# A Gram matrix from high and low parts: one fp32 product replaced by three fp32r products, with the splits placed on ScalarE and VectorE ahead of the edge plan

## What is computed

```
xn = _layernorm(x, axis=-1)
x = x + _L0_gnn_ref(xn, edge_index, ...) + _L0_mix_ref(xn[None], w_qkv, w_out, b_out)[0]

def _L0_mix_ref(x, w_qkv, w_out, b_out):
    qkv = x @ w_qkv
    ...
    attn = jnp.einsum('bhnd,bhmd->bhnm', q, k) * (SCALE / n)
    out = jnp.einsum('bhnm,bhmd->bhnd', attn, v)
    ...
    return out @ w_out + b_out
```

## Time and profile before

| what | value |
|---|---|
| median of 3 runs | 908.46 us (906.35 to 911.83) |
| the profiled execution's own time | 909.68 us |
| its span, first to last instruction | 907.9 us |
| mean granted TensorE clock | 0.951 |
| PE busy | 803.0 us, 88% |
| VectorE busy | 630.3 us, 69% |
| ScalarE busy | 372.4 us, 41% |

### The profile page before, as it was taken

The page is one execution under the profiler, slowest core; times in us unless marked ns, Lnnn a source line. Parts: engine busy times, 40 slices in busy tenths (PEclk is TensorE's granted clock), DMA queues, the critical chain, the costliest instruction groups (busy, mean ns, idle before and its releaser), DMA issues. The chain is left out here.

```text
span 907.9 us, 11554 instructions
## 1 busy us (share of the span) xinstructions
PE 803.0 (88%) x4058; PEld 575.9 (63%) x4058; DVE 630.3 (69%) x1207; ACT 372.4 (41%) x557; POOL 102.4 (11%) x76
## 2 busy tenths in 40 slices
PE   5999999999999960895899998998797999999788
PEld 3777888888778840563587777555463445446564
DVE  7667776776749557598853232778867888884976
ACT  2342343332313240475112117756315887884150
POOL 3000000000000005012280004443100000000010
PEclk9989999999999995898599999999898999999999
DMA  5571312210302414996311102000001000000002
GB/s 173 150 250 49 107 56 71 71 36 8 117 1 92 147 65 138 286 373 233 97 66 47 47 22 72 1 1 1 2 2 48 1 1 1 1 0 1 6 1 93
DMA packets 48152, 66.63 MB, mean 73 GB/s; under 512 B 4268, under 2 KB 22460, under 8 KB 48095
## 3 DMA queue, kind: packets, MB, share of 16 engines
q1 hardware_dynamic: 43903, 56.22, 19.4%
q0 software_dynamic: 2384, 6.92, 2.3%
q10 hardware_dynamic: 1808, 2.75, 0.8%
HBM read 56.38 MB, written 9.50 MB: 73 GB/s over the span
## 5 line engine op out<-in xcount | busy, mean ns | idle before, releaser
L879 PE MATMUL bank<-xT,slot 128*128 128x512 f32 (+1 forms) x248 | 105.9, 427 | 5.7 <-DVE xT L1626 5.7
L880 PE MATMUL bank<-xT,slot 128*128 128x512 f32 (+1 forms) x248 | 98.5, 397 | 0.0
L881 PE MATMUL bank<-xT,slot 128*128 128x512 f32 (+1 forms) x248 | 98.2, 396 | 0.0
L1350 ACT ACTIVATE slot<-bank 128x512 fp32r<-128x512 f32 (+3 forms) x60 | 34.2, 586 | 144.3 <-PE bank L1129 56.3
L879 PE MATMUL bank<-slot 128*128 128x512 f32 (+1 forms) x212 | 85.2, 402 | 4.1 <-issue 1.8
L2131 DVE TENSOR_REDUCE key<-bank 128x2 f32<-128x1024 f32 x64 | 75.2, 1218 | 14.5 <-PE bank L1189 14.5
L879 PE MATMUL bank<-slot,xT 128*128 128x512 f32 (+1 forms) x192 | 79.2, 412 | 3.7 <-DVE arena L2194 2.8
L881 PE MATMUL bank<-slot 128*128 128x512 f32 (+1 forms) x212 | 81.9, 386 | 0.0
L880 PE MATMUL bank<-slot 128*128 128x512 f32 (+1 forms) x212 | 81.8, 386 | 0.0
L881 PE MATMUL bank<-slot,xT 128*128 128x512 f32 (+1 forms) x192 | 77.0, 401 | 0.0
L1563 ACT ACTIVATE arena<-bank 128x1024 f32<-128x1024 f32 x64 | 65.7, 1027 | 27.7 <-PE bank L1255 27.6
(11 more groups left out here) (323 smaller groups left out, 1647.5 us busy)
## 6 DMA issues: line engine op xcount, KB each, us to landing
arena<-in_ewT SPq DMA_DIRECT2D x16, 1024.0 KB, 11.5
arena<-in_edge_attr SPq DMA_DIRECT2D x16, 512.0 KB, 4.0
wraw<-in_qkvT SPq DMA_DIRECT2D x3, 1024.0 KB, 5.2
expert_rows<-rows SPq DMA_DIRECT2D x1, 2560.0 KB, 14.0
wraw<-in_L_ffn_expert_b POOLq DMA_DIRECT2D x16, 160.0 KB, 5.8
expert_results<-wraw ACTq DMA_DIRECT2D x16, 160.0 KB, 5.7
xn<-in_x SPq DMA_DIRECT2D x4, 512.0 KB, 6.3
wraw<-in_L_mix_w_qkv SPq DMA_DIRECT2D x2, 1024.0 KB, 7.8
```

Source lines behind the costliest of these rows:

```text
L879: pe.matmul(out, L[1], R[0], start=start, stop=False, **kw)
L880: pe.matmul(out, L[0], R[0], start=False, stop=False, **kw)
L881: return pe.matmul(out, L[0], R[1], start=False, stop=stop, **kw)
L1350: act.activation(h, src, kw.pop("func", ACT.Copy), **kw).then_inc(hi_done, 1)
```

## The change

A tile `xn_split` (high and low part of the normalised input, 128 x 2 x 8 x 512 fp32r) is laid over a part of the arena that is empty at that time. ACT copies each normalised tile into its high half, between and behind its square roots. DVE subtracts it for the low half: the pairs 0 and 1 inside the loop of moments, the pairs 2 and 3 after the last `normalise`, ahead of the edge plan. PE waits for a tile's low part before that tile's share of G, and makes the share in three fp32r passes with `mm3`. The transposes still read `xn`.

```
+        xn_hl = nc.alloc_sbuf_tensor_at("xn_split", [P, 2, T, D], F32R, offset=arena_at + 4 * AW)
...
             for t in range(T):
                 turn_rows(0, t)
+                pe.wait_ge(gram_lo, t + 1)
                 for m in range(C):
                     if t == 0:
                         open_bank("G", m)
-                    ins = pe.matmul(at("G", m)[:, m * P:D], xn[:, t, chunk(m)], xn[:, t, m * P:D], start=t == 0, stop=t == T - 1)
+                    ins = mm3(at("G", m)[:, m * P:D], [xn_hl[:, v, t, chunk(m)] for v in range(2)],
+                              [xn_hl[:, v, t, m * P:D] for v in range(2)], t == 0, t == T - 1)
...
-            for g in range(len(GROUPS[0])):
-                deviation(0, g)
+            for g in range(len(GROUPS[0]) + 1):
+                if g < len(GROUPS[0]):
+                    deviation(0, g)
+                for t in range(2 * g - 2, 2 * g) if g else ():
+                    act.wait_ge(xn_ready, t + 1)
+                    act.activation(xn_hl[:, 0, t, :], xn[:, t, :], ACT.Copy).then_inc(gram_hi, 1)
...
+            def gram_low(g):
+                for t in range(*GROUPS[0][g]):
+                    dve.wait_ge(gram_hi, t + 1)
+                    dve.tensor_tensor(xn_hl[:, 1, t, :], xn[:, t, :], f32(xn_hl)[:, 0, t, :], ALU.subtract).then_inc(gram_lo, 1)
+
             for t in range(T):
                 dve.wait_ge(x_in[t // 2], 16)
                 link(moments(t, xn[:, t, :]))
...
                     if t > 2:
                         normalise(0, t // 2 - 1, lambda t: xn[:, t, :])
+                    if t > 4:
+                        gram_low(t // 2 - 2)
             normalise(0, 3, lambda t: xn[:, t, :])
+            gram_low(2)
+            gram_low(3)
             dve.wait_ge(ids_in, 48)
```

More of the change, by code:

```diff
@@ L508, in build @@
         xn_ready = sem("xn_ready")
+        gram_hi = sem("gram_hi")
+        gram_lo = sem("gram_lo")
         masked = sem("masked")
```

## The result

| what | before | changed |
|---|---|---|
| first measurement: median of 10 executions each | 906.74 us | 910.20 us (908.34 to 912.44) |
| ratio, 95% interval | | 1.0031 [1.0017, 1.0045], +2.8 us |
| second measurement (12 of the changed kernel, 29 of before) | 907.25 us | 910.3 us, 1.0033 [1.0021, 1.0044] |
| span of the profiled execution | 907.9 us | 910.2 us |
| GT starts (profiled execution) | 35.27 us | 37.10 us |

A forecast was written before the change was run, and what follows sets the result against it. PE, busy 88% of the span, was taken to bound the kernel. Bank 0's wait of +3.0 us, less 0.87 and 0.19 from cheaper shares, gave +1.9 on the median of 908.46: 910.4 us, range 906.2 to 914.2.

The forecast's parts named there:

- DVE's queue: Eight low-part subtractions ahead of DVE's edge plan delay it and the emptying of bank 0 by 4.9 us, at most 5.5.
- The wait for bank 0: Tile 4's transposes wait for DVE's low part of xT 0, starting at about 27.25 us, 3.0 later than before.
- The share: A tile's share of G on PE in three passes costs 1.87 us, at most 2.03, instead of 2.16 in fp32.
- Hidden costs: Spans and DMA issues for mWv and mWo move 4.9 us later with DVE's queue, yet arrive before they are wanted.
- The sum: At GT's start: 3.0 - 0.87 - 0.19 = +1.9 us, so 37.2 instead of 35.27; up to +3.0 with dearer prices.
- The slow start: PE's first share starts at 15.05 instead of 11.79, at the lower clock until 21.0; bank 0's wait swallows both.
- B: Rival: PE alone, not bank 0, decides tile 4's start; -0.7 us at G's end, 907.8 us; chance 0.05.
- C: Rival: PE's 3 us gap behind the first transposes makes the clock rise much later; up to +15 us, 923; chance 0.04.
- E: Rival: a later wait for a DMA that does not move absorbs the delay; 908.5 us; chance 0.07.
- D: Rival: the 2 us shift removes or adds a low-clock stretch elsewhere; 907.5 or 913.3 us; chance 0.05 each way.

The follow-up runs named there:

- fp32 kept: Changed kernel with splits, waits and order kept, but PE multiplies plain fp32 xn instead of three passes; 1.0053 against before, +4.8 us.
- one pass: Changed kernel with only the high by high pass of the Gram matrix, splits and waits kept; one execution, 908.6 us.
- the queue alone: Kernel before plus eight unused 128x512 DVE subtractions between the last normalise and the edge plan, Gram matrix still fp32; 1.0086, +7.8 us.
- the version on POOL: Changed kernel with the eight low parts subtracted by POOL instead of DVE, ahead of its wait for the spans; 1.0026 against before, +2.4 us.

## Why the prediction was right, and the step that was too small

- **DVE's queue.** 4.9 us for eight subtractions; measured 4.82. The price per instruction that the prediction takes from the Trainium skill, "VectorE: DVE Perf Modes", section on the TRN2 errata, 5.5 us in all, was not the one.
- **The wait for bank 0.** Tile 4's transposes at 27.25; measured 27.20, in the changed kernel, with fp32 kept and with one pass. With the queue alone 27.65, in an execution that began 0.3 us late.
- **The share.** 1.87 us was worked out; measured 1.95, since the first 512-wide pass behind the transposes takes 0.31 us and not 0.23 and the 384-wide ones 0.18. The transposes became 0.05 us shorter, so that a tile is 2.33 us instead of 2.30. Three tiles gained 0.80 us where 0.87 was in the sum, and the last tile 0.30 where 0.19 was: two misses that cancel, by luck.
- **Hidden costs.** The spans and mWv moved by about 5 us, mWo's issue by 6.0 (25.39 to 31.43), and no row waits for them; ACT's copies lie in its idle time. These covers held.
- **The sum.** GT at 37.2; measured 37.10. +1.9 against that one profile; measured +1.83, that is 2.93 - 0.80 - 0.30.
- **The slow start was called hidden "whatever PE does until then".** True of the changed kernel. But the sum set it against one profile of before, in which the clock rose late (the first share took until 16.06, the second started at 16.91). In the others tile 2 started up to 1.3 us earlier. That step, the before side of the subtraction, was mis-sized: by the four profiles the sum should have said +1.8 to +3.2 at GT, centred on 2.5. The share of 4.3 us in the earlier trace rows, twice 2.16, showed that the clock rose only behind it there; what was missing was the thought that the change takes away PE's freedom to profit from an early rise.
- **Rivals.** B, C and E did not come about: PE did wait at tile 4, its clock was up by about 19.5, and the executions' times show the loss. D is real in both directions: both profiles of the changed kernel lack the low clock at 130 to 145 us, and the two have spans of 910.2 and 905.8 us with GT at the same time. L1976, at 340.99 in the first, starts at 338.69 in the second, whose window from 320 to 330 us has a clock of 1.00. The forecast held although D moved single executions by as much as the whole effect.
- **Not weighed for this wait.** The new wait before tile 4 could itself bring the clock down. The clock fell behind the waits of 4.07, 2.34 and 6.04 us, not behind those of 0.36, 1.04, 1.52 and also not behind 2.35 us (the version on POOL). The wait before M is 1.8 us in all fourteen profiles; the matmul behind it takes 0.76 or 0.77 us in seven and 0.47 in the other seven. So the length of the wait alone does not decide. Whether some executions of the changed kernel lose more that way, and so make up the rest between 2.5 and 2.8 to 3.0 us, is open; neither of its two profiles shows it, and the intervals hold 2.5.

## What to carry to other kernels

Before making an engine's work cheaper, find the next wait on its path and count what the helpers of the change add in front of that wait's releaser: here 1.1 us of cheaper matmuls behind the wait stood against 3 us of queue before it. If the helper work must be paid, put the releases that others wait for ahead of it, and leave the first tiles, whose operands are just arriving, on the path that needs no preparation; that turned +2.8 into -1.5 us. And when the effect is a few microseconds, take several profiles of the kernel before, since one of them may hold a late clock that the change would appear to win back.

## What the runs showed of the hardware

- Three fp32r passes cost 0.77, 0.54, 0.36 and 0.28 us for 512, 384, 256 and 128 columns in tile 4 of the changed kernel, 1.95 us in all; the plain fp32 share is 2.16 us at full rate. With transposes 0.05 us shorter, the gain is 0.26 us of a tile's 2.59. Of two consecutive 128-wide passes the starts stand 0.11 us apart, nearly the 0.12 of a 256-wide one.
- POOL's subtraction of 128x512 took 1.25 to 1.36 us on average. Some DVE instructions that started during one ended with it (L1650 on two columns, L1673 and L1674 on one); L1644, on 512 columns, was not held.
- The start of tile 2 differed by up to 1.3 us between executions with the same first start, by the moment at which PE's rate doubled. Behind a wait of 2.3 us the clock fell in one kernel and not in another, and behind the same 1.8 us before M the first matmul was slow in half of the profiles.
